# Reordering the work of a slot, and spreading 48 instead of 36 attention batches over the adjacency read

## The reference

```python
# layer 0: one masked product per edge kind
o1 = matmul((adj == 1), matmul(V, w1)); o2 = ... (adj == 2) ... w2; o3 = ... (adj == 3) ... w3
x = layernorm(x + o1 + o2 + o3 + bias)
# layer 1: attention over the edges, h = X @ W.T + b
e = h @ we1 + be1 + (h @ we2 + be2).T
e = where(e >= 0, e, 0.01 * e)
attention = softmax(where(adj > 0, e, -9e15), axis=1)
x = layernorm(x + attention @ h)
```

## Time and profile before

| | us |
|---|---|
| median of three runs (1709.4 to 1712.68) | 1710.22 |
| the profiled execution, time | 1715.92 |
| its span | 1714.3 |
| TensorE busy with matmuls | 1461.9 (85%) |
| VectorE busy | 1140.8 (67%) |
| ScalarE busy | 959.5 (56%) |
| GpSimd busy | 206.0 (12%) |

### The profile page before, as it was taken

One profiled execution on the slowest core, in us unless ns is written; L12 is line 12 of the kernel. 1 busy time (PEld: TensorE's weight loads), 2 busy tenths in 40 slices (PEclk: granted clock), 3 DMA queues, 4 the chain that ended last, 5 costly groups with the idle time before them and its releaser, 6 DMA issues. The chain is left out here.

```text
span 1714.3 us, 19415 instructions
## 1 busy us (share of the span) xinstructions
PE 1461.9 (85%) x6934; PEld 672.6 (39%) x6934; DVE 1140.8 (67%) x2384; ACT 959.5 (56%) x1454; POOL 206.0 (12%) x188
## 2 busy tenths in 40 slices
PE   3677787896997997997988589999999999999996
PEld 1323343342443443443434234444444444444443
DVE  4557767777697696786776576556566666666563
ACT  2223422633364445444434566777888787888774
POOL 1113213123122120121120220000000000000000
PEclk9889898898998998998998789999999999999998
DMA  9999889879788888788892210000001100000100
GB/s 117 120 125 98 93 83 108 93 73 106 86 86 100 74 93 100 73 92 94 76 106 34 62 37 7 25 1 25 26 25 40 35 25 25 25 25 25 32 1 14
DMA packets 122436, 106.46 MB, mean 62 GB/s; under 512 B 4768, under 2 KB 114912, under 8 KB 122336
## 3 DMA queue, kind: packets, MB, share of 16 engines
q0 software_dynamic: 67584, 67.12, 43.5%
q1 hardware_dynamic: 54752, 38.05, 7.8%
HBM read 294.39 MB, written 12.09 MB: 179 GB/s over the span
## 5 line engine op out<-in xcount | busy, mean ns | idle before, releaser
L960 ACT ACTIVATE neg_masks<-e_row,cols 128x512 int8<-128x512 f32 x1024 | 640.7, 708 | 214.4 <-PE ps L1156 149.3
L1156 PE MATMUL ps<-pos_masks,tables 128*128 128x512 fp8e4 x2048 | 623.4, 387 | 69.0 <-DVE pos_masks L589 64.3
L1156 PE MATMUL ps<-neg_masks,tables 128*128 128x512 fp8e4 x2048 | 621.1, 385 | 0.0
L1110 PE MATMUL ps<-edge_masks,tables 128*128 128x512 fp8e4 (+1 forms) x2048 | 475.9, 393 | 49.7 <-DVE edge_masks L568 34.1
L587 DVE TENSOR_TENSOR neg_masks<-pos_masks,neg_masks 128x2048 uint16<-128x2048 uint16 x128 | 158.5, 1238 | 281.5 <-ACT neg_masks L960 280.5
L1156 PEld LDWEIGHTS ps<-pos_masks,tables 128*128 128x128 f16 x2048 | 196.6, 99 | 325.8 <-issue 114.7
L1110 PEld LDWEIGHTS ps<-edge_masks,tables 128*128 128x128 f16 x2048 | 204.2, 101 | 306.2 <-DVE edge_masks L568 37.5
L1156 PEld LDWEIGHTS ps<-neg_masks,tables 128*128 128x128 f16 x2048 | 203.3, 99 | 251.7 <-issue 17.5
L568 DVE TENSOR_SCALAR edge_masks<-edges 128x512 uint16<-128x512 uint16 x512 | 110.4, 290 | 147.7 <-ACT edges L951 147.5
L945 ACT ACTIVATE packed_bf<-packed 128x1024 bf16<-128x1024 uint8 x64 | 67.4, 1053 | 250.4 <-DVE packed L558 250.4
L548 DVE TENSOR_TENSOR seen<-seen,adj_in 128x2048 uint16<-128x2048 uint16 x128 | 164.4, 1285 | 25.9 <-DMA adj_in<-adj 19.1
(11 more groups left out here) (115 smaller groups left out, 615.5 us busy)
## 6 DMA issues: line engine op xcount, KB each, us to landing
adj_in<-adj POOLq DMA_DIRECT2D x128, 512.0 KB, 11.8
e_row<-e_scratch SPq DMA_DIRECT2D x30, 256.0 KB, 4.2
edges<-x SPq DMA_DIRECT2D x8, 512.0 KB, 14.1
x_rows<-x SPq DMA_DIRECT2D x8, 512.0 KB, 5.4
x_scratch<-x SPq DMA_DIRECT2D x8, 512.0 KB, 9.1
edge_masks<-x_scratch SPq DMA_DIRECT2D x16, 256.0 KB, 3.2
out<-adj_in SPq DMA_DIRECT2D x16, 256.0 KB, 2.6
part_scratch<-a_c_rows SPq DMA_DIRECT2D x14, 256.0 KB, 5.0
```

The lines of the kernel that those rows point to most:

```text
L960: ins = e.activation(GN[:, n:n + GR].bitcast(I8), e1row[:, q % 2, :], ACT.Sign, bias=t2[:, JC * c + j:JC * c + j + 1])
L1110: ins = e.matmul(ps[:, h, :], v_hl[:, i, JC * c + j, :], U0[:, n:n + GR].bitcast(kind), start=c == 0 and j == 0 and i == 0, stop=c == NCH ...
L1156: ins = e.matmul(z_bank(q, k), tab[:, c, 2 * k + i, j, :], mask[:, n:n + GR].bitcast(F8A), start=first and j == 0 and i == 0, stop=final a ...
```

## The change

Four things are changed together.

1. `plan()` takes its segments from a table `EARLY`. Block 1 and 2 of it also fetch column 1 and column 2 for row groups 0 and 1 (segments of a single batch), and from block 3 on each segment has four columns instead of three. 48 batches come before the ordinary order; 44 of them lie in slots below 64 (33 before), and from slot 28 to the end every slot has one. `START` goes from 5 to 4: a block's first row group begins a slot sooner after its scores.
2. The order in a slot: VectorE does the masks and the collecting before the packing; ScalarE makes the gates of slot k+1 at the end of slot k, after convert and edges; TensorE turns in the middle of the batch, after 16 of its 32 matmuls.
3. The tail: the scores' sums move from off 3 to 2, the turning from 4 to 3, the tables from 5 to 4; GpSimd does its tail work ahead of the slot's loads instead of behind them.
4. Partial sums: `PRIOR` and `ADDS` let a row group be interrupted twice. There are 34 segments instead of 30, 18 stores and 18 reads of partial sums instead of 14 of each, and the buffer for a part that is read has its own place (it was in the edge masks').

```diff
-START = 5
+START = 4
+EARLY = {
+    0: [(0, [0]), (1, [0])],
+    1: [(2, [0, 1]), (0, [1]), (1, [1]), (3, [0, 1])],
+    2: [(4, [0, 1, 2]), (0, [2]), (1, [2]), (5, [0, 1, 2])],
+    3: [(6, [0, 1, 2, 3]), (7, [0, 1, 2, 3])],
...
+PRIOR = [max([p for p in range(q) if SEGS[p][0] == SEGS[q][0]], default=None) for q in range(NQ)]
+ADDS = [q for q in range(NQ) if PRIOR[q] is not None]
...
 # VectorE
+                for m in at(k):
+                    masks(m)
+                    after(m)
                 if k < K:
                     check_and_pack(k)
...
-                for m in at(k):
-                    masks(m)
-                    after(m)
...
-                    if off == 3:
+                    if off == 2:
                         e_sums(S)
 # ScalarE
-                for m in at(k):
-                    gates(m)
-                    after(m)
                 if k < K:
                     convert(k)
                     edges_of(k)
...
+                for m in at(k + 1):
+                    gates(m)
+                    after(m)
 # TensorE
+                for m in at(k):
+                    batch(m, 0)
                 if k < K:
                     turn(k)
+                for m in at(k):
+                    batch(m, 1)
+                    after(m)
 # GpSimd
-                for h in range(2):
-                    if 2 <= k + 2 < K:
-                        load(k + 2, h)
                 for S, off in tails(k):
...
+                for h in range(2):
+                    if 2 <= k + 2 < K:
+                        load(k + 2, h)
 # SyncE, for each early segment q
+                    if q:
+                        part_store(q - 1)
+                    part_load(q)
```

More of the change, by code:

```diff
@@ L81 @@
 NSLOT = SLOTS[-1] + 1
-assert LOWS == 2 * NS - 2 and NB == 128
+assert NB == 128
 def at(k):
@@ L137, in build @@
         out_sb = [ob0, ob1]
-        part_in = [U0[:, 2048 * n:2048 * (n + 1)].bitcast(F32) for n in range(2)]
+        parts = sb("part_in", [P, 2, GR], F32)
+        part_in = [parts[:, n, :] for n in range(2)]
         x1_in = [U0[:, 2048 * (n + 2):2048 * (n + 3)].bitcast(F32).rearrange("p (t d) -> p t d", d=D)
@@ L504, in _ @@
                         e_products(S)
-                    if off == 4:
+                for n, slot in enumerate(AGAIN):
+                    if k == slot:
+                        table_products_again(n)
+                for S, off in tails(k):
+                    if off == 3:
                         ones_column(S)
@@ L1030, in _ @@
             for k in range(NSLOT):
+                if k < NCH:
+                    split_high(k)
                 for S, off in tails(k):
@@ L1033, in _ @@
                         sd_of(S)
-                if k < NCH:
-                    split_high(k)
-                for m in at(k):
-                    gates(m)
-                    after(m)
+                        x1_of(S)
+                    if off == 3:
+                        e1_turned(S)
+                        b_d_of(S)
+                    if off == 4 and (S < 4 or S == NS - 1):
+                        high(S, yT8, xg[:, :, :])
+                for n, slot in enumerate(AGAIN):
+                    if k == slot + 1:
+                        e.wait_ge(s_l0, 2 * K)
+                        high(4 + n, xr_b, xr[n])
                 if k < K:
@@ L1046, in _ @@
                         y_of(S)
-                    if off == 2:
-                        x1_of(S)
-                    if off == 4:
-                        e1_turned(S)
-                        b_d_of(S)
-                    if off == 5:
-                        if S < 4 or S == NS - 1:
-                            high(S, yT8, xg[:, :, :])
-                for n, slot in enumerate(AGAIN):
-                    if k == slot + 1:
-                        e.wait_ge(s_l0, 2 * K)
-                        high(4 + n, xr_b, xr[n])
+                for m in at(k + 1):
+                    gates(m)
+                    after(m)
             for m in range(NB, NB + AFTER):
@@ L1142, in e1_turn, with batch @@
                 e.transpose(ps[0:RB, 3, 0:P], e1c[:, JC * S:JC * (S + 1)], idf).then_inc(s_e1T, 1)
-            def batch(m):
+            def batch(m, half):
                 q, g, c, first, final = BATCH[m]
-                e.wait_ge(s_lo, c + 1)
-                if first:
-                    ge(e, s_ev, q - 1)
-                    if q == 0:
-                        e.wait_ge(s_setc, 1)
-                e.wait_ge(s_pos, m + 1)
-                for j in range(JC):
+                if half == 0:
+                    e.wait_ge(s_lo, c + 1)
+                    if first:
+                        ge(e, s_ev, q - 1)
+                        if q == 0:
+                            e.wait_ge(s_setc, 1)
+                    e.wait_ge(s_pos, m + 1)
+                for j in range(JC // 2 * half, JC // 2 * (half + 1)):
                     n = 4096 * (m % 2) + GR * j
@@ L1200, in _ @@
                 for S, off in tails(k):
-                    if off == 1:
-                        o_of(S)
+                    if off == 3:
+                        e1_turn(S)
                 if 1 <= k <= K:
@@ L1205, in _ @@
                         layer0(k - 1, h)
+                for m in at(k):
+                    batch(m, 0)
                 if k < K:
                     turn(k)
+                for m in at(k):
+                    batch(m, 1)
+                    after(m)
+                for S, off in tails(k):
+                    if off == 0:
+                        o_of(S)
                 if k == 3:
                     weights()
-                for S, off in tails(k):
-                    if off == 4:
-                        e1_turn(S)
-                for m in at(k):
-                    batch(m)
-                    after(m)
                 if k == K + 6:
```

84 lines of the change are left out of this document (40 added, 44 removed), and 3 rows, old and new, of the table EARLY.

## The result

| | before | after |
|---|---|---|
| median of four runs, us | 1711.45 (1709.4 to 1715.55) | 1751.01 (1750.04 to 1758.73) |
| the profiled execution, us | 1715.92 | 1750.46 |
| its span | 1714.3 | 1748.8 |
| stage A (slots 8 to 27) | 277.2 | 316.7 |
| stage B (slots 28 to 63) | 539.3 | 627.1 |

The changed kernel is slower, ratio 1.0248 with a 95% interval of 1.0231 to 1.0266 (the quotient of the two medians is 1.0231). The forecast was 1738, its range 1675 to 1768. Stages B and C came out as summed (627.8 and 691.0), A 7.1 us longer (309.6).

What follows compares the result with a forecast made beforehand. Full slots during the read were taken as bound by a 15.16 us loop through VectorE and ScalarE, not TensorE's 14.26. 1715.9 + 32.4 + 88.5 - 92.6 = 1744.2, less 5.7 for the profiled run: 1738 us, range 1675 to 1768.

Steps and rivals of the forecast that it cites:

- stage A: End of slot 7's packing to slot 27's: eight batches instead of six, summed at 309.6 against 277.2 us, +32.4.
- stage B: Slot 27's packing to slot 63's: 36 full slots plus extras, summed at 627.8 us, 88.5 above 539.3.
- Stage C: From slot 63's packing to the span's end: 84 batches left instead of 95, summed at 691.0 us, -92.6.
- The loop of a slot: Convert, turn, evacuate, next batch's gates, AND, XOR, next packing: 15.16 us per full slot, above TensorE's 14.26.
- The end of a segment: On top of a slot: exponents 0.76 us, collecting 2.0 in the next, 0.7 more where a partial sum is added.
- off 0 to 1: Tail step: `y_of` ahead of the gates and the product by w1 on TensorE add 1.2 us.
- off 2: Tail slot: `rs_of`, square root, scale, bias and spread add 2.75 us, GpSimd's score product meeting the packing 4.1.
- The store wait: Single-batch segments' exponents wait for the store just issued: 6.45 us each in slots 13, 22, 24, 31, 32.
- That the batches fit under the read: Rival: A and B keep their lengths, only C shrinks, 1617.6 us; chance 0.17.
- Tops hidden: Rival: the loop holds but store waits (32 us) and GpSimd collisions (21.5) cost nothing, 1685 us; chance 0.12.
- Starvation: Rival: loads wait behind GpSimd's tail work in 16 slots, some 30 us, 1768 us; chance 0.16.
- TensorE's clock: Rival: waits lower the clock, ten slots costing some 20 us; kept inside the forecast's upper end, no separate chance.

Runs made afterwards that it cites:

- the fastest version: Changed kernel with gates ahead of the conversion, SyncE's x-row reload one partial store later and no single-batch segments: 1664.74 us, ratio 0.9736 to the kernel before.

## Why the prediction was right, and where it was not

- **The loop of a slot.** Summed 15.16, measured 15.09, with TensorE waiting 0.66 for the conversion (I had said near 1). Shown: taking the gates out of it gave 14.26 in a plain slot and 50.5 us in B, some 30 of them by the plain pace alone.
- **The end of a segment, off 0 to 1, off 2.** In B a block of eight slots was summed at 134.8 and measured 134.7, 136.4 and 136.5; off 2 at 22.0, and it took 21.9 to 22.1, though the square root held VectorE 4.71 us: in a plain slot 2.45 of that is the wait for the gates, and the rest with `rs_of`'s own 0.37 is 2.6, for 2.75 summed. "SBUF — State Buffer" of the Trainium skill, section "SBUF: two separate sides", has the ports shared by VectorE and GpSimd as an exclusive lock, held for a whole instruction. The trace agrees: the second `seen` step was held until GpSimd's first product ended, the first shift-and-or until the second ended (rows of slot 42), and the XOR of slot 48 in the experiment with packing first lost 2.30 of GpSimd's 2.35. What the prediction made of the page, up to 6.6 us, was wrong: a product's 3.3 us hold some 1.0 of its own waiting for VectorE, and alone it takes 2.34 (before, at 268.05 us). Two such products cost 4.1, as the sum had it from the earlier trace rows; so the row agreed with the page and was no exception to it.
- **The store wait: mis-sized.** Term 6.45 for each of five, measured 2.05, so 22 us less: 13.2 in A, 8.8 in B. The mechanism and the slots were right. What I took for the price of a store was that of a store close behind the adjacency loads (see below).
- **SyncE's queue: the term that was missing.** I followed the reload's place in the last stage but not in slots 13 and 21, where store and next row stand behind it. In slot 13 it is the row that comes late, and it cost 8.2: 3.8 above the sum and the 4.4 that the cheaper store wait had left over. In slot 21 it is the store, and it cost 6.3: the sum of 17.9 had a collecting in it that lies in slot 20, and without it is 15.9. The experiment with the later reload took 7.2 and 6.4 off.
- **Stage A.** 7.1 us longer: slots 13 and 21 +8.1, slots 18 to 20 +3.4, slot 25 +1.9 (21.0 for 19.1), slots 22 and 24 -5.8 (the store waits alone would make -8.8), the others within 1.4. Of the 3.4 in slots 18 to 20, 2.0 is the collecting that the sum had put into slot 21. That the stage came within 7.1 is partly luck: 13.2 us too much for three store waits stand against 14.5 of the queue that was left out.
- **Stage B.** The hit of 0.7 is partly luck: 8.8 too much for two store waits stand against small tops too low, among them off 4 (17.7 for 17.16), slot 28 (21.0 for 17.2), off 3 (16.2 for 15.16) and off 1 of the last two blocks (17.5 for 16.36). The last is the clock: slot 41 took 16.1 at a granted clock of 1.00, slot 49 17.5 with 0.55 from 803 to 806 us.
- **Stage C.** Batch 50 started 81.3 us behind slot 63's packing (I took 83). The 77 batches behind it took 589.2 with their segment ends, 7.65 each, for 578.3 + 8.5; the end 20.6.
- **The subtraction of 5.7.** I carried over that the profiled run of before lay 5.7 above its median. After's profiled run (1750.46) lies at its median. The sum itself, 1744.2, is 6.3 below it, of which 7.1 is stage A. This offset belongs to one execution and not to the kernel.
- **The rivals.** That the batches fit under the read: refuted by the changed kernel, and shown in part once the gates are ahead (B 556.2, against 521 at best). Tops hidden: the store waits shrank but were not hidden, the rest stands in the rows. Starvation: 5.5 us at most. TensorE's clock: 0.96 in B for 0.95; the average is right and hides that slots 49 and 57 lost 1.4 us each to it.

What stays open: whether two buffers for a segment's sums would remove the store wait, and what a `START` of another value does in the fastest version. Neither was tried there. A version in the old order with `START = 6` and 44 early batches was written to see whether the late row of scores is what holds a slot up in each block (expected: 1650 us if it is, 1675 if not); its engines end up waiting for one another, a deadlock, so it has no time and that question stays open too. The fastest version's slots of off 4 still take 17 to 19.7 us. Its trace shows that their gates, which the edit leaves behind the evacuation, keep them in the old loop: in slot 44 the evacuation starts at 637.72, the gates at 638.63, the masks at 643.73, and the packing behind them ends at 652.9. With a collecting the loop gives 17.2; no run takes the rest apart.

## What to carry to other kernels

Before an in-order queue is rearranged, write down the loop that goes once round all engines for one slot and add it up from rows: here 15.16 against TensorE's 14.26 decided the time, while no engine was busy for more than 9 tenths of the stage. A part of a change may be good and another bad: the table gave 1.5% and the order took 3.5%, and only separate runs show that the turning in the middle of the batch was worth keeping (30 us, with the gates ahead) and the place of the gates was not. Look what stands ahead of a store or a small load on its queue too, since a reload that waits for a buffer holds everything behind it.

## What the hardware showed unexpectedly

- **A partial store lands late when it is issued close behind an adjacency load.** This is the time from its issue to the exponents that wait for it, over all fourteen kernels that have a trace. Issued 11.7 us or more behind the last load it took 2.0 to 2.2 us (23 cases; one more, at 11.9 us, took 3.8), at 9.3 to 11.6 us 2.6 to 4.3 (5), and at 4.7 to 8.2 us 6.0 to 7.8 (17). At 2.2 us it took 13.8 to 14.1 (5, all in slot 21); these have a second cause beside them, since the 512 KB reload of `x_rows` is issued 0.4 us ahead of the store on the same queue. A load's own landing takes 11.8 us at the median. So the store seems to wait out what is left of the load, and the price of my term was set by the distance. GpSimd's load and SyncE's store, before, slot 14:

```profile
209.93 1.48 POOL L445 DMA_DIRECT2D adj_in<-adj  x2 [18.86 <-DVE packed L558]
...
215.25 0.33 SPq L345 DMA_DIRECT2D part_scratch<-a_c_rows  x1
```

and in the changed kernel, slot 22:

```profile
324.55 1.49 POOL L458 DMA_DIRECT2D adj_in<-adj  x2 [20.67 <-DVE packed L572]
...
336.46 0.32 SPq L355 DMA_DIRECT2D part_scratch<-a_c_rows  x1
```

The old order issues the loads behind a packing that comes just ahead of the collecting, so the store follows them by 5 us. In the new order the packing comes last, the store goes ahead of it, and the last loads are 12 us old. This was read from where the cases lie; no run moved a store alone, so the cause is argued and not shown.
- **GpSimd holds up more of VectorE than the packing's last steps, and it holds it for its whole instruction.** A VectorE step with two inputs in SBUF that starts under a GpSimd product or addition ends about its own length behind it. The second `seen` step ended at 700.6, 1.1 us behind the product's 699.55; the first shift-and-or at 703.90, 1.1 behind 702.82; the XOR of slot 48 at 769.03, 1.1 behind 767.94; and in the earlier trace rows the first shift-and-or at 625.58, 1.1 behind 624.50. Alone each of these steps takes 1.2 to 1.3 us. So nearly all of a step's work comes after GpSimd has finished, and the run with the loads first moved the meeting from one slot to the next without removing it. GpSimd waits in its turn: its product takes 2.34 us when it starts ahead of the VectorE step and 3.3 when it starts under one.
- **Some waits in a busy stretch were followed by TensorE at the lower clock level, and the average clock does not show it.** In stage B of the changed kernel TensorE waited for the conversion 3.7 us or more eight times, and each time its next pairs of matmuls started 0.85 us apart instead of 0.43. Of seven waits between 2.2 and 2.6 us three were followed by the same. Slot 49, where the wait was 2.26:

```profile
802.96 0.77 PE L1134 MATMUL ps<-idb,packed_bf 128*128 128x128 bf16 x8 [2.26 <-ACT packed_bf L959]
803.52 1.06 PE L1169 MATMUL ps<-pos_masks,tables 128*128 128x512 fp8e4 x2
804.37 1.06 PE L1169 MATMUL ps<-neg_masks,tables 128*128 128x512 fp8e4 x2
```

In slot 41 the wait was 2.40 and the pairs stayed 0.43 apart, and in the plain slots, with waits of 0.66, they did too. The price is that of the matmuls that fall into it: 1.4 us in slot 49, 1.7 in slot 48 of the run with the packing first, 2.8 in its slot 51.
